# An NVFP4 MLP beside an ALiBi attention: weights turned by the crossbar instead of TensorE

## The chip, the cores and the metric

One core of one Trainium2 chip. The time is device microseconds of one execution. The profile is one more execution, and its trace names engines PE (TensorE), PEld (its weight loads), DVE (VectorE), ACT (ScalarE), POOL (GpSimd) and SP (SyncE, which here only issues transfers; SPq is its queue).

## The reference

x is 2048 x 512 in float32. It is normalised by layer norm to xn. The output is x + attention(xn) + mlp(xn). Attention has 16 query heads of 32 columns on 4 key and value heads, causal, with ALiBi slopes, softmax, and a projection Wo with a bias. The MLP has 4096 hidden columns; its three weight matrices come as 4-bit codes, two to an int32 word, with a float32 scale for each 32 columns:

```python
Wg = dequant_nvfp4(gate_W_packed, gate_scales)      # 4096 x 512
Wu = dequant_nvfp4(up_W_packed, up_scales)          # 4096 x 512
Wd = dequant_nvfp4(down_W_packed, down_scales)      # 512 x 4096
gate = jnp.einsum('th,nh->tn', xt, Wg)
up = jnp.einsum('th,nh->tn', xt, Wu)
gelu = jnp.tanh(0.7978845608028654 * (gate + 0.044715 * gate ** 3)) * gate * 0.5 + gate * 0.5
out = jnp.einsum('tn,hn->th', gelu * up, Wd)
```

## The kernel before, in words

**Numbers in two parts.** Matmuls of the MLP run in float16. A float32 value is held as a rounded part and the rest behind it (hi and lo, as in wh and wl, xh and xl, ih and il, phi and plo), and a product takes three matmuls: hi x hi, hi x lo, lo x hi. Attention scores run on float32 rows.

**Preamble** (function `preamble`). It normalises x, turns it, projects q, k and v in four chunks c of 512 tokens with five projections j each (j = 0 is k, 1 to 4 are q), stores them in DRAM, reads the scales, and decodes, turns and splits the first group of MLP weights. Its decode steps stand at (c, j) = (2, 4), (3, 0) and (3, 2). SP's program there is one sequence: the part stores of each projection (L538, L539), the v stores (L510), the loads for the first head (L499 to L503), and last the column scales (L554). The main loop begins when every engine has ended the preamble.

**Main loop** (function `main_loop`). 16 turns, called heads here: a turn i does attention head i and one group of 256 of the 4096 MLP columns. A head has 48 slots, and each engine walks through the slots by its own list, in order. The tables at the top say what stands in which slot. On TensorE a slot s holds: a score block (L1267, slots 6 to 44, `SCORE_AT`), up to two blocks of row maxima (L1245, up to slot 25), two halves of three MLP matmuls each (`PIECES`: gate, gate, down, up, up, down, L1213 and L1233), and in some slots a batch of probabilities times values (`VALUES_AT`, L1276: slots 12, 20, 28, 32, 40 and 47). The score blocks of slots 29 to 44 belong mostly to the last chunk of queries.

**The chain behind a score.** score_ps is one bank. TensorE writes it, DVE masks it where it lies on the diagonal, ACT takes the exponential into p (L1395, three buffers, `PR = 3`, so the exp of a block waits until POOL has read p of three blocks before), ACT rounds it to phi (L1402), and POOL subtracts to plo (L1668). The values batch of a slot waits for phi and plo of all its blocks; the batch of slot 47 for those of slot 44. POOL does, besides the plo splits: il (L1676, behind each up block, in slots 5, 11, ... 47), two adds of attention parts (L273, slots 19 and 23), their normalising (L279, slot 36) and onl (L291, slot 39).

**Weights of the next group.** In head i, group i + 1 is prepared. raw words are loaded by SP at the end of head i - 1 (L311). DVE decodes matrix m (0 gate, 1 up, 2 down) in five steps, one a slot, from slots 26, 31 and 36 (`DECODE_FROM`): two shifts (L319, L322), one mask over 1024 words (L326), and two multiplications by the scales (L334), which write wf, float32, 128 x 1024. There is one wf, so matrix m + 1 may write it only when m has been read. Then, in the slots of `TURN_W_AT` (31, 32, 36, 37, 41, 42), TensorE turns half of wf with four transposes of 128x128 (L347) into one of the two banks that the maxima used before, ACT copies it to wh (L354), and DVE subtracts to wl (L359). wh and wl have two buffers, one for each parity of i. The last head prepares nothing; DVE and ACT scale and split Wo there (ACT at slots 31 to 34).

```python
def turn_weights(pe, m, a, before, maxima):
    ...
    for k in range(KT):
        at = a * C + k * P if m < 2 else k * GROUP + a * P
        mm = nc.tensor.transpose(banks[a][:, k * P:(k + 1) * P], wf[:, at:at + P], ident[:])
    mm.then_inc(wturn_done, 1)
```

**SP in a head**: load_v and load_k for the next head; then for each chunk c, behind the last score block of the chunk: load_q of the next head (L1094, L1096) and gather_o of chunk c - 1 (L1151 to L1156), with the steps of the row sums at c = 0, 1 and 2 (spread_recips, L263, at c = 2); then load_raw for group i + 2, store_on and gather_o of the last chunk. The last block of chunk 2 is in slot 29, that of chunk 3 in slot 44. ACT copies o_ps and l_ps of a chunk (L1415, L1418), and lraw, of which there is one, waits for the store of the chunk before.

## Time and profile before

| what | value |
|---|---|
| median of 3 runs | 1736.85 us (1735.28 to 1737.32) |
| profiled execution | 1738.06 us |
| its span in the trace | 1736.2 us |
| busy: TensorE, VectorE, ScalarE, GpSimd | 1666.9, 1312.1, 1067.0, 935.9 us |
| preamble | up to about 123 us of the span |
| main loop, 16 heads | about 97 us each |
| middle head that is read closely | 707.2 to 804.5 us of the span |

The profile gives busy times by engine, groups of like instructions by line, who waited for whom, the chain that ended last, and a timeline. Matmuls overlap in it: a record of TensorE is longer than the time to the next one, so costs on TensorE are read from start to start.

### The profile page before, as it was taken

How to read it: one execution, taken by the hardware profiler on the slowest of the kernel's cores; microseconds unless marked ns; L12 is line 12 of the kernel's file. 1: busy time of each engine (PE TensorE's matmuls, PEld its weight loads, DVE VectorE, ACT ScalarE, POOL GpSimd, SP SyncE). 2: the span in 40 equal slices, each digit the busy share in tenths (PEclk: the TensorE clock that was granted, in tenths of full speed). 3: DMA queues.
4: the chain of work that ended last, by engine and by line, in shares of the span. 5: the costliest groups of instructions: out<-in, count | busy, mean ns of one | idle time of the engine just before them, and what ended most of it. 6: DMA issues, size and time to landing. Idle time of an engine off the chain costs nothing.

```text
span 1736.2 us, 30755 instructions
## 1 busy us (share of the span) xinstructions
PE 1666.9 (96%) x10337; PEld 830.9 (48%) x10337; DVE 1312.1 (76%) x2782; ACT 1067.0 (61%) x1788; POOL 935.9 (54%) x807
## 2 busy tenths in 40 slices
PE   4989999999999999999999999999999999999998
PEld 3764444444444444444444444444444444444443
DVE  6767778777777777777777778777777778777755
ACT  2336757575666757575766757575767657575650
POOL 3304637465665747465655747464656647464650
PEclk9999999999999999999999999999999999999999
DMA  6761020202021020202021020202020120202135
GB/s 195 197 188 44 15 74 18 76 26 71 18 62 38 23 79 17 75 27 75 17 72 26 26 76 17 75 27 76 18 76 19 28 74 17 76 27 82 32 102 181
DMA packets 95843, 106.86 MB, mean 62 GB/s; under 512 B 38288, under 2 KB 63768, under 8 KB 93992
## 3 DMA queue, kind: packets, MB, share of 16 engines
q1 hardware_dynamic: 91368, 99.27, 20.6%
q10 hardware_dynamic: 4320, 5.64, 1.0%
q8 instruction: 83, 1.36, 0.3%
q14 instruction: 72, 0.59, 0.1%
HBM read 69.60 MB, written 22.42 MB: 53 GB/s over the span
## 4 chain that ended last, share of the span: by engine, by line
PE 74%; DVE 8%; issue 6%; ACT 5%; DMA 0%; POOL 0%; SPq 0%; POOLq 0%; DVEq 0%; ACTq 0%
PE up_ps L1233 16%; PE down_ps L1213 16%; PE gate_ps L1233 15%; PE o_ps L1276 8%; PE score_ps L1267 8%; PE max_ps L1245 4%; PE turn_ps L1245 3%; ACT p L1395 2%; DVE mxp L1526 2%; PE l_ps L1276 2%; ACT wh L354 1%; PE max_ps L347 1%; DVE score_ps L1511 1%; DVE gl L1482 1%; DVE acc L1473 1%
## 5 line engine op out<-in xcount | busy, mean ns | idle before, releaser
L1668 POOL TENSOR_TENSOR plo<-p,phi 128x512 f16<-128x512 f32 (+1 forms) x576 | 661.0, 1158 | 317.6 <-ACT phi L1402 316.3
L1395 ACT ACTIVATE p<-score_ps,pshift 128x512 f32<-128x512 f32 (+1 forms) x576 | 381.5, 662 | 284.3 <-DVE score_ps L1511 154.7
L1676 POOL TENSOR_TENSOR il<-prod,ih 128x512 f16<-128x512 f32 x128 | 160.4, 1253 | 371.1 <-DVE ih L1505 371.1
L1402 ACT ACTIVATE phi<-p 128x512 f16<-128x512 f32 (+1 forms) x576 | 349.5, 607 | 15.2
L1267 PE MATMUL score_ps<-qst,kst 128*128 128x512 f32 (+3 forms) x640 | 308.0, 497 | 20.5 <-ACT p L1395 18.8
L1526 DVE TENSOR_REDUCE mxp<-max_ps 128x1 f32<-128x512 f32 x256 | 175.5, 686 | 52.2 <-PE max_ps L1245 52.2
L1473 DVE TENSOR_TENSOR acc<-down_ps,acc 128x512 f32<-128x512 f32 x237 | 161.8, 683 | 62.4 <-PE down_ps L1213 62.1
L1233 PE MATMUL gate_ps<-xh,wh 128*128 128x512 f16 x512 | 198.8, 388 | 0.0
L1233 PE MATMUL up_ps<-xh,wh 128*128 128x512 f16 x512 | 197.9, 387 | 0.0
L1213 PE MATMUL down_ps<-wh,ih 128*128 128x512 f16 x506 | 195.8, 387 | 0.0
L1233 PE MATMUL gate_ps<-xh,wl 128*128 128x512 f16 x512 | 194.8, 380 | 0.0
L1233 PE MATMUL gate_ps<-xl,wh 128*128 128x512 f16 x512 | 194.7, 380 | 0.0
L1233 PE MATMUL up_ps<-xh,wl 128*128 128x512 f16 x512 | 194.0, 379 | 0.0
L1233 PE MATMUL up_ps<-xl,wh 128*128 128x512 f16 x512 | 194.0, 379 | 0.0
L1213 PE MATMUL down_ps<-wl,ih 128*128 128x512 f16 x506 | 191.8, 379 | 0.0
L1213 PE MATMUL down_ps<-wh,il 128*128 128x512 f16 x506 | 191.8, 379 | 0.0
L1267 PEld LDWEIGHTS score_ps<-qst,kst 128*128 128x128 f32 x640 | 116.3, 189 | 117.1 <-ACT p L1395 51.8
L1276 PE MATMUL o_ps<-phi,vst 128*32 128x512 f16 (+3 forms) x1744 | 164.4, 348 | 0.0
L1245 PE MATMUL max_ps<-kst,qst 128*128 128x512 f32 (+2 forms) x320 | 151.7, 474 | 11.9 <-SPq L1099 5.5
L1245 PE MATMUL turn_ps<-kst,qst 128*128 128x512 f32 (+3 forms) x320 | 141.3, 441 | 0.4 <-DVE mxp L1522 0.3
L1276 PE MATMUL o_ps<-plo,vst 128*32 128x512 f16 (+3 forms) x1024 | 136.2, 342 | 0.0
L1379 ACT ACTIVATE gl<-gate_ps,cur 128x512 f32<-128x512 f32 x128 | 87.7, 685 | 69.4 <-issue 44.0
(301 smaller groups left out, 2836.0 us busy)
## 6 DMA issues: line engine op xcount, KB each, us to landing
qst<-q_parts SPq DMA_DIRECT2D x192, 64.0 KB
o<-oraw SPq DMA_DIRECT2D x192, 64.0 KB, 2.0
kst<-k_parts SPq DMA_DIRECT2D x45, 256.0 KB, 6.0
vst<-v_parts SPq DMA_DIRECT2D x16, 512.0 KB, 6.1
q_parts<-o SPq DMA_DIRECT2D x24, 256.0 KB, 3.4
acc<-in_L_attn_x_dram SPq DMA_DIRECT2D x4, 1024.0 KB, 7.5
raw<-L_ffn_gate_W_packed_dram SPq DMA_DIRECT2D x16, 256.0 KB, 3.0
raw<-n_L_ffn_up_W_packed_dram SPq DMA_DIRECT2D x16, 256.0 KB, 3.1
```

Source lines behind the costliest of these rows:

```text
L1213: mm = nc.tensor.matmul(dst[:], lhs, rhs, start=(q == 0), stop=(q == 5))
L1233: mm = nc.tensor.matmul(dst[:], lhs, rhs, start=(q == 0), stop=(q == 11))
L1245: mm = nc.tensor.matmul(dst[:, 0:cols], qst[:, c, t * P:(t + 1) * P], kst[par][:, m * CH:m * CH + cols], start=True, stop=True)
L1267: mm = nc.tensor.matmul(score_ps[:, col:col + width], kst[par][:, j * P:(j + 1) * P], qst[:, c, tok:CH], start=True, stop=True, skip_group ...
L1276: mm = nc.tensor.matmul(bank[g * HD:(g + 1) * HD, tok:CH], vst[:, j, of * HD:(of + 1) * HD], src[n % PP][:, col:col + CH - tok], start=sta ...
L1379: nc.scalar.activation(gl[a][:], gate_ps[:], ACT.Square, scale=cur[par][:, a:a + 1]).then_inc(square_done, 1)
L1395: nc.scalar.activation(p32[n % PR][:, 0:cols], score_ps[:, 0:cols], ACT.Exp, bias=pshift[:, 0:1]).then_inc(exp_done, 1)
L1402: nc.scalar.activation(phi[n % PP][:, 0:cols], p32[n % PR][:, 0:cols], ACT.Copy).then_inc(phi_done, 1)
L1473: nc.vector.tensor_tensor(acc[:, n % NT, :], bank[:], before, ALU.add).then_inc(acc_done, 1)
L1526: nc.vector.tensor_reduce(mxp[c % 2][:, t, m:m + 1], pair_ps[n % 2][:, 0:cols], AX.X, ALU.max).then_inc(red_done, 1)
L1668: nc.gpsimd.tensor_tensor(plo[n % PP][:, 0:cols], p32[n % PR][:, 0:cols], phi[n % PP][:, 0:cols], ALU.subtract).then_inc(plo_done, 1)
L1676: nc.gpsimd.tensor_tensor(il[w % 2][:, a, :], prod[a][:], ih[w % 2][:, a, :], ALU.subtract).then_inc(il_done, 1)
```

## The change

The float32 transposes of the MLP weights on TensorE go, with the copies out of PSUM behind them. Instead, for each matrix, ACT rounds the whole wf (128 x 1024) to float16 rows, which lie in the raw buffer just decoded (`rows_hi`); POOL subtracts them from wf to the rows behind them (`rows_lo`), which lie in the second part of o3; and SP issues two transposing DMAs (`turn_rows`), one for the hi rows into wh and one for the lo rows into wl, each 256 KB. In the main loop ACT does this in slots 31, 36 and 41, POOL in slots 32, 37 and 42, SP behind spread_recips of chunk 2. There is one buffer of lo rows, so POOL waits for the turn of matrix m - 1 before it writes those of m. The decode of m + 1 waits for POOL's read of wf. TensorE waits for the turned weights at its first use in a head. The scale that the copies of the down weights applied moves into the product on DVE (L1497). The packed down weights are loaded in two DMAs, in another order of columns. In the preamble, ACT has its copies at (2, 4), (3, 1) and (3, 4), POOL its three subtractions behind all its other work, and SP the turns at (3, 1), (3, 3) and before the last v store.

```diff
-TURN_W_AT = {31: (0, 0), 32: (0, 1), 36: (1, 0), 37: (1, 1), 41: (2, 0), 42: (2, 1)}
+ROWS_HI_AT = {31: 0, 36: 1, 41: 2}
+ROWS_LO_AT = {32: 0, 37: 1, 42: 2}
+W_DMAS = 2
...
-TURN_FIRST_AT = {(3, 0): 0, (3, 2): 1}
+ROWS_FIRST_AT = {(2, 4): 0, (3, 1): 1, (3, 4): 2}
+TURN_FIRST_AT = {(3, 1): 0, (3, 3): 1}
...
+    hi_rows = [t[:].bitcast(F16) for t in raw]
...
+        for a in range(2):
+            src = packed[2].rearrange("(k p) (g a w) -> g a p k w", p=P, a=2, w=GROUP // 4)[bass.ds(g, 1), a]
+            sp.dma_start(raw[m][:].rearrange("p (a k w) -> p a k w", a=2, k=KT)[:, a],
+                         src.rearrange("o p k w -> (o p) k w")).then_inc(raw_in[m], 16)
...
                 dve.wait_ge(dec_step, before * 9 + m * 3 + 3)
-                dve.wait_ge(wturn_done, before * 6 + 2 * m)
+                if m or before:
+                    dve.wait_ge(rowlo_done, before * 3 + m)
...
-    def turn_weights(pe, m, a, before, maxima):
...
-    def weights_hi(act, m, a, before, b):
...
-    def weights_lo(dve, m, a, before, b):
...
+    def rows_hi(act, m, before):
+        act.wait_ge(wf_done, before * 6 + 2 * m + 2)
+        nc.scalar.activation(hi_rows[m], wf[:], ACT.Copy).then_inc(rowhi_done, 1)
+
+    def rows_lo(pool, m, before, lo_row):
+        pool.wait_ge(rowhi_done, before * 3 + m + 1)
+        nc.gpsimd.tensor_tensor(lo_row, wf[:], hi_rows[m], ALU.subtract).then_inc(rowlo_done, 1)
+
+    def turn_rows(sp, m, before, b, lo_row):
+
+        for done, rows, dst in ((rowhi_done, hi_rows[m], wh[b]), (rowlo_done, lo_row, wl[b])):
+            sp.wait_ge(done, before * 3 + m + 1)
+            sp.dma_start_transpose(dst[:, m].rearrange("p a (k n) -> p (a k) n", n=P), rows).then_inc(w_in[m], 16)
...
+                        if (c, j) in TURN_FIRST_AT:
+                            turn_rows(sp, TURN_FIRST_AT[c, j], 0, 0, lo_rows[TURN_FIRST_AT[c, j]])
...
+                turn_rows(sp, 2, 0, 0, lo_rows[2])
                 store_v(NCH - 1)
...
                 nc.gpsimd.partition_all_reduce(rall, rmax, P, RMAX).then_inc(rall_done, 1)
+                for m in range(3):
+                    rows_lo(pool, m, 0, lo_rows[m])
...
+        lo_rows = [o[:, 1, :].bitcast(F16) for o in o3]
...
                         if i and c == 2:
                             spread_recips(sp, i - 1)
+                        if i < LAST and c == 2:
+                            for m, used in enumerate((gate_done, up_done, down_done)):
+                                sp.wait_ge(used, after(i * (GU if m < 2 else ND)))
+                                turn_rows(sp, m, i + 1, 1 - par, lo_rows[1 - par])
                     if i + 2 < HEADS:
                         for m in range(3):
-                            sp.wait_ge(wf_done, (i + 1) * 6 + 2 * m + 2)
+                            sp.wait_ge(w_in[m], 16 * W_DMAS * (i + 2))
                             load_raw(sp, m, i + 2)
...
+                            if n % ND == 0:
+                                pe.wait_ge(w_in[2], 16 * W_DMAS * (g + 1))
...
+                                if n == 0:
+                                    pe.wait_ge(w_in[m], 16 * W_DMAS * (i + 1))
...
-                        if s in TURN_W_AT and i < LAST:
-                            m, a = TURN_W_AT[s]
-                            turn_weights(pe, m, a, i + 1, (red_done, after((i + 1) * NMAX)))
...
+                        if s in ROWS_HI_AT and i < LAST:
+                            rows_hi(act, ROWS_HI_AT[s], i + 1)
...
-                        nc.vector.scalar_tensor_tensor(prod[a][:], gl[a][:], 0.5 * IS / (XS * WS) ** 2, up_ps[:],
+                        nc.vector.scalar_tensor_tensor(prod[a][:], gl[a][:], cur[par][:, 4 + a:5 + a], up_ps[:],
...
+                        if s in ROWS_LO_AT and i < LAST:
+                            m = ROWS_LO_AT[s]
+                            if i:
+                                pool.wait_ge(osum_done, 2 * i)
+                            else:
+                                pool.wait_ge(acc_done, after(1))
+                            if m:
+                                pool.wait_ge(w_in[m - 1], 16 * W_DMAS * (i + 2))
+                            rows_lo(pool, m, i + 1, lo_rows[1 - par])
```

## Rows read from the trace of the kernel before

**Rows 1.** The page: busy time of each engine, share of the span, instructions
```profile
PE 1666.9 (96%) x10337; PEld 830.9 (48%) x10337; DVE 1312.1 (76%) x2782; ACT 1067.0 (61%) x1788; POOL 935.9 (54%) x807
```

**Rows 2.** The chain that ended last: start us, length us, what (longest pieces)
```profile
215.26 2.59 PE up_ps L1233 x12
...
1578.31 2.59 PE up_ps L1233 x12
1675.17 2.59 PE up_ps L1233 x12
```

**Rows 3.** Timeline of TensorE in one head's last third: start us, length us
```profile
768.40 0.38 PE L1213 MATMUL down_ps<-wh,il 128*128 128x512 f16 x1
...
768.85 0.39 PE L1233 MATMUL gate_ps<-xh,wh 128*128 128x512 f16 x1
...
771.48 0.38 PE L1233 MATMUL gate_ps<-xl,wh 128*128 128x512 f16 x1
771.69 0.60 PE L347 MATMUL max_ps<-ident,wf 128*128 128x128 f32 x4
...
772.37 0.39 PE L1213 MATMUL down_ps<-wh,ih 128*128 128x512 f16 x1
...
787.75 0.50 PE L1267 MATMUL score_ps<-qst,kst 128*128 128x512 f32 x1 [0.82 <-ACT p L1395]
...
802.61 0.39 PE L1276 MATMUL o_ps<-phi,vst 128*32 128x512 f16 x2
```

**Rows 4.** Busy by stretch: length, PE, PEld, DVE, ACT, POOL, clock, DMA; middle, last head
```profile
774.34:800.97 26.63, 25.50 (x156) 12.53 (x154) 21.49 (x32) 21.23 (x37) 21.39 (x17) 1.00 0.06 16
1652.12:1676.22 24.10, 22.72 (x130) 9.62 (x129) 11.86 (x21) 19.99 (x34) 19.48 (x17) 1.00 0.14 45
```

**Rows 5.** Groups of the whole run, shapes apart: the splits on GpSimd and ScalarE
```profile
L1668 POOL TENSOR_TENSOR plo<-p,phi 128x512 f16<-128x512 f32 x512 | 612.6, 1206 | 285.9 <-ACT phi L1402 284.6
...
L1402 ACT ACTIVATE phi<-p 128x512 f16<-128x512 f32 x512 | 322.8, 630 | 13.2
...
L1668 POOL TENSOR_TENSOR plo<-p,phi 128x256 f16<-128x256 f32 x64 | 49.7, 777 | 31.7 <-ACT phi L1402 31.7
...
L1402 ACT ACTIVATE phi<-p 128x256 f16<-128x256 f32 x64 | 26.7, 416 | 2.0
```

**Rows 6.** Timeline of ScalarE in the same stretch
```profile
770.58 0.69 ACT L1395 ACTIVATE p<-score_ps,pshift 128x512 f32<-128x512 f32 x1 [0.19 <-PE score_ps L1267]
...
773.15 0.59 ACT L354 ACTIVATE wh<-max_ps 128x512 f16<-128x512 f32 x1
...
775.72 0.69 ACT L1395 ACTIVATE p<-score_ps,pshift 128x512 f32<-128x512 f32 x1
```

**Rows 7.** Groups of VectorE with GpSimd busy (774.3 to 801)
```profile
L334 DVE TENSOR_TENSOR wf<-dec,sc 128x512 f32<-128x512 f16 x4 | 4.7, 1204 | 0.0
...
L326 DVE TENSOR_SCALAR dec<-dec 128x1024 int32<-128x1024 int32 x2 | 2.2, 1082 | 0.0
```

**Rows 8.** Groups of VectorE with GpSimd idle (96 to 116)
```profile
L334 DVE TENSOR_TENSOR wf<-dec,sc 128x512 f32<-128x512 f16 x6 | 3.9, 689 | 0.1
...
L326 DVE TENSOR_SCALAR dec<-dec 128x1024 int32<-128x1024 int32 x3 | 2.1, 695 | 0.1
```

**Rows 9.** Timeline of the transfer queue at the preamble's end
```profile
107.46 1.75 SPq L539 DMA_DIRECT2D q_parts<-o  x1
109.25 2.25 SPq L510 DMA_DIRECT2D v_parts<-wh  x4
...
122.38 0.46 SPq L554 DMA_DIRECT2D column_scales<-acc  x1
```

**Rows 10.** Timeline of ScalarE at the preamble's end, in brackets its wait
```profile
116.31 0.60 ACT L717 ACTIVATE o<-proj 128x512 fp32r<-128x512 f32 x1 [3.85 <-DMA q_parts<-wl]
```

**Rows 11.** Transfers by line: size and median us to landing
```profile
o<-oraw SPq DMA_DIRECT2D x192, 64.0 KB, 2.0
...
acc<-in_L_ffn_up_scales_dram SPq DMA_DIRECT2D x1, 256.0 KB, 14.3
```

More of the change, by code:

```diff
@@ L215, in build @@
             wf_done = sem("wf_done")
[L216 to L218 removed]
+            rowhi_done = sem("rowhi_done")
+            rowlo_done = sem("rowlo_done")
+            w_in = [sem(f"w_turned{m}") for m in range(3)]
             preamble(nc, locals())
@@ L470, in preamble @@
         CLEARED = 3
-        load_raw, decode_step, turn_weights, weights_hi, weights_lo = weight_steps(nc, e, w_ps)
+        load_raw, decode_step, rows_hi, rows_lo, turn_rows = weight_steps(nc, e)
+        lo_rows = [t.bitcast(F16) for t in sraw]
         QSCALE = float(np.float32(1 / np.sqrt(np.float32(HD))))
@@ L724, in _ @@
                             root(c + 2)
-                        if (c, j) in TURN_FIRST_AT:
-                            for a in range(2):
-                                weights_hi(act, TURN_FIRST_AT[c, j], a, 0, 0)
+                        if (c, j) in ROWS_FIRST_AT:
+                            rows_hi(act, ROWS_FIRST_AT[c, j], 0)
                     act.wait_ge(v_sum, c + 1)
@@ L897, in _ @@
                                 decode_step(dve, DECODE_FIRST_AT[c, j], step, 0, 0)
-                for a in range(2):
-                    weights_lo(dve, 2, a, 0, 0)
                 values_lo(NCH - 1)
@@ L1023, in main_loop @@
         out_done = sem("out_done")
-        load_raw, decode_step, turn_weights, weights_hi, weights_lo = weight_steps(nc, e, pair_ps)
+        load_raw, decode_step, rows_hi, rows_lo, turn_rows = weight_steps(nc, e)
         (load_sums, row_sums, store_recips, spread_recips, add_parts, normalise, output_hi, output_lo
@@ L1102, in _ @@
                     sp.wait_ge(stored, 32 * NCH)
-                for m in range(3):
-                    load_raw(sp, m, 1)
                 def body(i, par, pair):
@@ L1114, in body @@
                     if i == 0:
+                        for m in range(3):
+                            sp.wait_ge(w_in[m], 16 * W_DMAS)
+                            load_raw(sp, m, 1)
                         sp.wait_ge(os_out, 16)
@@ L1167, in load_early @@
                     sp.wait_ge(wf_done, 6 * HEADS)
-                    sp.wait_ge(wturn_done, 6 * HEADS)
+                    sp.wait_ge(rowlo_done, 3 * HEADS)
+                    for turned in w_in:
+                        sp.wait_ge(turned, 16 * W_DMAS * HEADS)
                     for g in range(KVH):
```

78 lines of the change are left out of this document (19 added, 59 removed).

## The prediction

> **What bounds the kernel now.** I read the page first, then the chain, then one head's last third on each engine, then the preamble's end. On the page TensorE is busy 96% of the span [rows 1], so it looks like the bound everywhere, and the change takes work from it. The chain shows one mark per head, twelve up matmuls in a row: from 215.26 to 1578.31 there are 14 heads, 97.36 us each [rows 2]. The head behind them, the last, decodes and turns no weights, and still takes 96.86 us from mark to mark [rows 2]. So leaving the transposes out is not worth what they cost by themselves, unless the last head's own extras ate it. The reader should look for the engine that takes over. The timeline of TensorE shows it: at 787.75, between slots that hold the transposes, it sat idle 0.82 us for the exp on ScalarE [rows 3], and that exp may only run when GpSimd has read the p buffer of three blocks earlier (PR = 3). In the stretch from GpSimd's split of slot 32 to that of slot 44, 26.63 us, GpSimd is busy 21.39, TensorE 25.50 [rows 4]. This third of the head is where all added work goes; the other two thirds are untouched.
>
> **Removed from TensorE.** From the last matmul of slot 30 (768.40) to the first of slot 31 (768.85) pass 0.45 us, a score block between them. With four transposes as well, 771.48 to 772.37, it is 0.89 [rows 3]. A group of four costs 0.44 us (not the 0.60 of its record, which overlaps its neighbours). Six groups are 2.64 us a head, 15 heads 39.6 us. That is the ceiling of the gain. The six wl subtractions leave VectorE, which does not set this stretch's end; I count nothing for them. GpSimd is what may cover them.
>
> **Moved on ScalarE.** The two wh copies out of PSUM, 0.59 each [rows 6], become one copy of 128x1024 in SBUF. By the phi rows 256 more columns cost 630 - 416 = 214 ns [rows 5], so 1024 cost 630 + 428 = 1.06 us: the sum stays. But it all stands in slot 31, ahead of phi, where before half of it stood two slots later: phi and exp of slots 32 and 33 (exp at 775.72 [rows 6]) come 0.5 us later, and GpSimd's split of slot 32 starts at 774.84, not 774.34.
>
> **Added on GpSimd.** rows_lo has the form of the plo split at twice the width. 512 columns take 1206 ns, 256 take 777 [rows 5]: 1024 take 1206 + 2 x 429 = 2.06 us by slope, 2.41 by doubling; I take 2.2, so 6.6 us a head, all in slots 32, 37 and 42. Behind it queue the plo splits, and behind these the exps, the scores and, at slot 47, the last batch of values, which needs the plo of slot 44. TensorE began that batch at 802.61 [rows 3]. Today's GpSimd work of the stretch and the new: 21.39 + 6.6 = 28.0 us, from 774.84: plo 44 ends at 802.8. Without the transposes TensorE would be there at 802.61 - 2.64 = 799.97 and wait. So GpSimd becomes the bound, and the batch starts 0.2 us later than before.
> The lower bound takes GpSimd undisturbed, as in the last head, where the same 17 operations took 19.48 us [rows 4], and rows_lo at 2.06: 774.84 + 25.7 = 800.5, 2.1 us earlier. The upper bound comes from the decode. Beside GpSimd a wf multiply of VectorE takes 1204 ns and a mask 1082 [rows 7], alone 689 and 695 [rows 8]; GpSimd in turn pays 21.39 - 19.48 = 1.9 us. The decode steps of the stretch are 4 x 0.69, 2 x 0.70 and two shifts; with the shifts at no more than a mask each, 5.6 us. If GpSimd paid all of them: 19.48 + 5.6 + 3 x 2.41 = 32.3, end 807.1, 4.5 us later. Today GpSimd has 5.2 idle microseconds in the stretch for them to hide in; with no gaps left the 1.9 grows to some 1.9 / 0.8 = 2.4, which is +0.5 on the 0.2. The decode also waits for rowlo now, and rows_hi for the decode. I take +1.0 us a head, 15 us in all, nearest the sum of today's rows.
> The Trainium skill, "SBUF — State Buffer", section Who interferes with whom, has VectorE's two-port operations and GpSimd hold one port pair by turns for a whole instruction, the loser blocked. The trace agrees that both stretch, but shows GpSimd paying about a third of VectorE's length; by the rule in full the sum would be the upper bound above, 67 us instead of 15.
>
> **Added on the transfer queue.** Six transposing DMAs a head, issued by SP behind spread_recips. Issue: 0.46 to 1.75 us for one today [rows 9]; I take 0.6, and 0.46 to 1.75 for the range. Six are 3.6 us in a stretch in which SP only waits for scores. Behind the last of them stand load_q, gather_o and load_raw of the head's end; ScalarE's lraw copy waits for gather_o, and some microseconds at a head's start are free there. The down weights' load, now two DMAs, hides there too. TensorE's new waits for turned gate and up weights stand at a head's start, over 10 us behind slot 37's rows; the one for down weights stands eight slots into the head, so a turn issued at 803 has some 15 us. Landing: no row shows a transposing DMA. Between SBUF tiles 64 KB land in 2.0 us, and 256 KB in small pieces take 14.3 [rows 11]. GpSimd's rows_lo of m = 1 (slot 37, about 788) waits for the turn of m = 0, whose rows are ready at 778: up to some 9.5 us cost nothing, and I take that it is less, as a contiguous SBUF copy is the nearest.
> Two pages of the skill disagree here. "DMA: Bandwidth & Descriptors", section Latency and other measured facts, gives transposing DMAs 261 GB/s, an estimate of 1.0 us for 256 KB, which hides. "VectorE: DVE Perf Modes", section The three transpose paths, gives the crossbar 1309 ns for a 128x128 block against 390 on TensorE; eight blocks in a row would be an estimated 10.5 us for each DMA, which does not hide. No run here shows either.
>
> **The preamble.** Its end is set by SP, not TensorE: v stores, 4 in 2.25 us from 109.25, the last issue at 122.38 [rows 9], and ScalarE waited 3.85 us for a store before 116.31 [rows 10]. The 24 transposes there save nothing. Added: two turns at 0.6 us before the store that ScalarE waits for (+1.2, 117.5), its copy 0.5 behind that (1.06, to 119.1), rows_lo 2.2 (121.3), one turn (121.9), the v stores and the column store (2.7): 124.6 instead of 122.84, +1.8. At 1.75 us an issue, all six in SP's chain of 10.7 us of other work from 109.2: 130.4, +7.6. I take +4.
>
> **Sum.** 15 + 4 = +19 us. The profiled execution took 1738.06 (span 1736.2), 1.2 above the median of 1736.85; on the median's scale I forecast 1756.
>
> **Rivals.**
> Faster: GpSimd keeps up as in the last head. For it: 19.48 against 21.39 [rows 4], and fewer VectorE operations. Against: the last head has no decode, which now meets more GpSimd work. It gives 4 - 15 x 2.1 = -28, 1709; the ceiling is 4 - 39.6, 1701. It decides from where the added work costs GpSimd less than 802.61 - 774.84 - 21.39 = 6.4 us a head beyond today's, less 0.3 for the preamble's 4 us over 15 heads. Chance 0.23.
> Ports by turns: the upper bound, 4.5 a head, 67 + 4 to 8: about 1805; half of it 1775. For it: the record of wf grows by 0.5 us beside GpSimd. Chance 0.17 for +2.5 a head and more.
> Slow crossbar: a landing over 9.5 us. At 14.3, rows_lo of m = 1 starts at 792.4, ends at 794.6, lands at 808.9, rows_lo of m = 2 ends at 811.1, two plo 1.8: 812.9, +10.3 a head, near 1895. The 10.5 us of the skill's page, with hi and lo in a row, would give about 16 us a head, near 1980. Chance 0.10.
>
> **The numbers.** Forecast case (-0.5 to +2.5 us a head, 1733 to 1778) 0.50. A measurement of this kernel tells about 0.2%, 3.5 us. Faster takes the first rival and a sliver of the forecast case: 0.25. Same, 1733 to 1740, 0.08. Slower 0.67. The range leaves out the slow crossbar and the fastest tenth: 1715 to 1805.
>
> **What would show it.** Right: head marks 98 to 99 us apart; GpSimd without a gap in slots 32 to 44; a TensorE wait before the values of slot 47, named plo; rows_lo of 2.1 to 2.4 us. Wrong: marks at 95 us (GpSimd kept up), a GpSimd wait for a DMA on wh or wl at slots 37 and 42 (crossbar), SP issues of several microseconds, or TensorE waiting for gate weights at a head's start.

## The result, and the profile after

The changed kernel takes **1756.17 us** (median of 4 runs, 1754.83 to 1757.97) against 1736.76 for the kernel before on the same chip: ratio 1.0115, interval 1.0099 to 1.0131. It is 19 us slower. The profiled execution took 1755.9 us (span 1754.1); the trace of it splits the loss in two. One execution of the copy with the down rows at slot 45 took 2338.73 us at a mean granted clock of 0.656, and its median below leaves that one out.

The page after: busy time of each engine, the transfer queues, the chain that ended last by engine.

```profile
PE 1643.9 (94%) x9953; PEld 787.8 (45%) x9953; DVE 1274.1 (73%) x2686; ACT 1067.2 (61%) x1740; POOL 1043.9 (60%) x855
...
DMA packets 205666, 132.00 MB, mean 75 GB/s; under 512 B 156304, under 2 KB 173592, under 8 KB 203816
...
issue 42%; POOL 36%; PE 11%; DVE 2%; ACT 1%; POOLq 0%; DMA 0%; SPq 0%; DVEq 0%; ACTq 0%
```

TensorE has 384 instructions and 23 us of busy time less than in [rows 1], GpSimd 48 instructions and 108 us more. 36% of the chain that ended last is now GpSimd's. The number of DMA packets more than doubled (before 95,843).

The same marks of that chain as in [rows 2], and one more: the twelve up matmuls of the first head and of the last, and the up_ps of the final projection; in the second fence the last mark in the kernel before.

```profile
222.78 2.59 PE up_ps L1236 x12
...
1693.39 2.59 PE up_ps L1236 x12
...
1745.67 2.59 PE up_ps L1336 x12
```
```profile
1727.80 2.59 PE up_ps L1337 x12
```

In the kernel before, the first stands at 215.26 [rows 2]. So the first mark comes 7.5 us later, and the loop (first to last mark) takes 1522.89 us against 1512.54, **+10.35 us, 0.69 a head**. All the experiments below are read by this one difference; the times of whole kernels are compared with their own runs of the kernel before. The first mark stands near the end of the first head, so that head's own transposes and subtractions lie ahead of it.

The 7.5 us are there when the loop begins. The first matmul of the loop, in the kernel before and in the changed one:

```profile
123.62 0.45 PE L1245 MATMUL max_ps<-kst,qst 128*128 128x128 f32 x1 [5.51 <-SPq L1099]
```
```profile
131.19 0.45 PE L1248 MATMUL max_ps<-kst,qst 128*128 128x128 f32 x1 [8.37 <-SPq L1091]
```

Each stands 0.78 us behind the end of SyncE's last issue of the preamble, at 122.84 and 130.41. From there to the first mark pass 91.64 and 91.59 us.

One head, from one start of the last batch of values to the next, and in the second line the stretch from GpSimd's split of slot 32 to that of slot 44. First the kernel before, then the changed one; the columns are those of [rows 4].

```profile
705.29:802.61 97.32, 95.85 (x612) 46.43 (x611) 74.98 (x161) 64.12 (x107) 56.59 (x48) 1.00 0.17 46
```
```profile
716.75:814.83 98.08, 94.45 (x588) 43.74 (x588) 72.74 (x155) 64.14 (x104) 63.35 (x51) 1.00 0.27 62
786.17:814.68 28.51, 25.36 (x139) 10.52 (x137) 20.88 (x28) 20.84 (x34) 28.15 (x20) 1.00 0.31 55
```

TensorE is busy 1.40 us a head less and idle 2.16 more (3.63 against 1.47), which makes the 0.76 of this head. ScalarE's busy time is unchanged. GpSimd is busy 6.76 us more, and in the stretch it is busy 28.15 of 28.51 us, where it was 21.39 of 26.63 [rows 4]. The granted clock is at 1.00 in both, and plays no part in the loop.

The idle times of TensorE in this head, in brackets, with what ended them:

```profile
788.29 0.50 PE L1270 MATMUL score_ps<-qst,kst 128*128 128x512 f32 x1 [0.83 <-ACT p L1394]
795.68 0.49 PE L1270 MATMUL score_ps<-qst,kst 128*128 128x512 f32 x1 [0.95 <-ACT p L1394]
799.72 0.50 PE L1270 MATMUL score_ps<-qst,kst 128*128 128x512 f32 x1 [0.41 <-ACT p L1394]
807.46 0.51 PE L1270 MATMUL score_ps<-qst,kst 128*128 128x384 f32 x2 [0.47 <-ACT p L1394]
814.83 0.39 PE L1279 MATMUL o_ps<-phi,vst 128*32 128x512 f16 x2 [0.62 <-POOL plo L1662]
```

The kernel before had two such waits in this stretch, 0.82 [rows 3] and 0.31. The last line is the batch that [rows 3] shows without a wait at 802.61: now it waits for plo. Part of GpSimd's timeline leading up to it:

```profile
803.02 1.61 POOL L294 TENSOR_TENSOR onl<-o,onh 128x512 f16<-128x512 f32 x1
804.59 2.90 POOL L1662 TENSOR_TENSOR plo<-p,phi 128x512 f16<-128x512 f32 x2
807.46 1.16 POOL L1670 TENSOR_TENSOR il<-prod,ih 128x512 f16<-128x512 f32 x1
808.58 2.26 POOL L1662 TENSOR_TENSOR plo<-p,phi 128x512 f16<-128x512 f32 x2
810.82 2.12 POOL L353 TENSOR_TENSOR o<-wf,raw 128x1024 f16<-128x1024 f32 x1
812.91 1.77 POOL L1662 TENSOR_TENSOR plo<-p,phi 128x512 f16<-128x512 f32 x2
```

Not one line has a bracket: nothing is waited for. (In the whole stretch GpSimd has one gap, 0.36 us before an il at 792.92.) The subtraction of 810.82 stands right ahead of the plo that the batch needs.

The groups of the added work (busy, mean ns | idle before, releaser), and the transposing transfers with their median time to landing:

```profile
L342 DVE TENSOR_TENSOR wf<-dec,sc 128x512 f32<-128x512 f16 x96 | 110.2, 1162 | 29.8 <-POOL o L353 29.2
L353 POOL TENSOR_TENSOR o<-wf,raw 128x1024 f16<-128x1024 f32 x45 | 96.4, 2143 | 0.0
...
L349 ACT ACTIVATE raw<-wf 128x1024 f16<-128x1024 f32 x48 | 50.6, 1054 | 22.5 <-DVE wf L342 22.5
```
```profile
wh<-raw SPq DMA_TRANSPOSE x48, 3.1
...
wl<-o SPq DMA_TRANSPOSE x45, 2.8
```

The subtraction takes 2.14 us, ScalarE's copy 1.05. Two new waits have come with them: VectorE stands 29.2 us before wf until GpSimd has read the old one, ScalarE 22.5 us before its copy until VectorE has written wf (4.4 of them once, in the preamble).

### The profile page after: what moved, and what is told of

The parts are those of the page before. It is cut to its first block, busy times and chain, and to the rows that moved or that the text cites. A ratio compares the mean times of both kernels' runs of the same rounds, so it can differ in the third digit from the quotient of the medians.

```text
span 1754.1 us, 29968 instructions
## 1 busy us (share of the span) xinstructions
PE 1643.9 (94%) x9953; PEld 787.8 (45%) x9953; DVE 1274.1 (73%) x2686; ACT 1067.2 (61%) x1740; POOL 1043.9 (60%) x855
## 4 chain that ended last, share of the span: by engine, by line
issue 42%; POOL 36%; PE 11%; DVE 2%; ACT 1%; POOLq 0%; DMA 0%; SPq 0%; DVEq 0%; ACTq 0%
POOL plo L1662 28%; POOL o L353 2%; PE o_ps L1279 2%; PE down_ps L1214 2%; PE up_ps L1236 2%; PE gate_ps L1236 2%; POOL il L1670 2%; POOL o L276 1%; POOL onl L294 1%; PE score_ps L1270 1%; POOL o L282 1%; PE max_ps L1248 1%; DVE mxp L1522 0%; PE turn_ps L1248 0%; PE l_ps L1279 0%
## 5 line engine op out<-in xcount | busy, mean ns | idle before, releaser
L1662 POOL TENSOR_TENSOR plo<-p,phi 128x512 f16<-128x512 f32 (+1 forms) x576 | 671.1, 1178 | 250.3 <-ACT phi L1401 250.3
L1270 PE MATMUL score_ps<-qst,kst 128*128 128x512 f32 (+3 forms) x640 | 313.7, 506 | 43.4 <-ACT p L1394 41.7
L1507 DVE TENSOR_TENSOR score_ps<-score_ps,mask_st 128x128 f32<-128x128 f32 x256 | 69.2, 293 | 94.1 <-PE score_ps L1270 92.8
```

What stands on the lines that cost most here:

```text
L1270: mm = nc.tensor.matmul(score_ps[:, col:col + width], kst[par][:, j * P:(j + 1) * P], qst[:, c, tok:CH], start=True, stop=True, skip_group ...
L1507: last = nc.vector.tensor_tensor(score_ps[:, col:col + P], score_ps[:, col:col + P], mask_st[:], ALU.add)
L1662: nc.gpsimd.tensor_tensor(plo[n % PP][:, 0:cols], p32[n % PR][:, 0:cols], phi[n % PP][:, 0:cols], ALU.subtract).then_inc(plo_done, 1)
```

## The experiments

**Theory G**: GpSimd's nearly gapless train between slots 32 and 44 sets the loop. **Rivals**: H, the handing over of the one wf buffer between VectorE, ScalarE and GpSimd; S, the transfers and SyncE's queue. Ratios are to the kernel before on the same chip; "loop" is the difference of the marks to the kernel before's 1512.54 us.

| kernel | ratio | median us | loop |
|---|---|---|---|
| changed | 1.0115 [1.0099, 1.0131] | 1756.17 | +10.35 |
| subtraction on VectorE | 1.0045 [1.003, 1.006] | 1743.99 | +0.64 |
| subtraction of 16 columns | 0.9933 [0.9917, 0.9949] | 1724.49 | -19.98 |
| before, no transposes | 0.9942 [0.9927, 0.9957] | 1725.95 | -9.91 |
| before, subtraction added | 1.0033 [1.0022, 1.0043] | 1741.34 | +4.89 |
| down rows at slot 45 | 1.0071 [1.0054, 1.0088] | 1746.21 | +0.77 |
| preamble order | 1.0107 [1.0091, 1.0122] | 1752.69 | +10.54 |
| transposes twice | 1.0262 [1.0247, 1.0277] | 1779.81 | +15.40 |
| output split at 45, 46 | 1.0049 [1.0032, 1.0066] | 1741.65 | +0.29 |
| three edits together | 1.0046 [1.0034, 1.0059] | 1743.42 | +1.55 |
| the same, up rows on VectorE | 1.0046 [1.0032, 1.006] | 1743.23 | -0.21 |
| before, output split at 45, 46 | 0.9958 [0.9944, 0.9972] | 1729.20 | -7.28 |
| copies a slot later | 1.006 [1.0047, 1.0074] | 1749.89 | +9.13 |

What TensorE waits for over the whole run, in us, sorts these kernels:

| kernel | for exponentials | for plo | for wf |
|---|---|---|---|
| before | 18.8 | 0 | 0 |
| changed | 41.7 | 8.7 | 0 |
| subtraction on VectorE | 39.9 | 0 | 0 |
| subtraction of 16 columns | 20.9 | 0 | 0 |
| before, no transposes | 35.2 | 0 | 0 |
| before, subtraction added | 19.4 | 0 | 3.7 |
| down rows at slot 45 | 42.5 | 0 | 0 |
| output split at 45, 46 | 40.6 | 0 | 0 |
| before, output split at 45, 46 | 11.0 | 0 | 0 |

### The low rows on VectorE

```diff
                         if s in DECODE_AT:
                             decode_step(dve, *DECODE_AT[s], nxt, i + 1)
+                        if s in ROWS_LO_AT:
...
+                            rows_lo_dve(dve, m, i + 1, lo_rows[1 - par])
...
-                        if s in ROWS_LO_AT and i < LAST:
...
-                            rows_lo(pool, m, i + 1, lo_rows[1 - par])
```

> The changed kernel with rows_lo in the main loop on VectorE instead of GpSimd, in the same slots (32, 37, 42); the preamble's three stay on GpSimd. Theory G (GpSimd's three subtractions of 2.14 us make it the bound of a head's last third): GpSimd gets its gaps back, the wait of the values of slot 47 for plo goes, heads take 95 to 96.5 us instead of 98.0, and with the preamble's +7.5 us left in place the time is 1705 to 1730, likeliest 1717. Rival H (the hand-over of wf, one buffer between four engines, holds the decode and with it ScalarE, whoever subtracts): 1745 to 1756. Rival S (the transposing DMAs or the transfer queue): no change, 1753 to 1759.

The loop comes back to within 0.6 us of before, and the batch of values waits no more, so where the subtraction runs was the loss. Theory G had asked for 1705 to 1730 us, though, and got 1744: VectorE pays. The group, three of its instructions in one head, and what GpSimd did beside the first:

```profile
L357 DVE TENSOR_TENSOR o<-wf,raw 128x1024 f16<-128x1024 f32 x45 | 77.0, 1711 | 0.0
```
```profile
779.47 1.22 DVE L357 TENSOR_TENSOR o<-wf,raw 128x1024 f16<-128x1024 f32 x1
788.76 2.29 DVE L357 TENSOR_TENSOR o<-wf,raw 128x1024 f16<-128x1024 f32 x1
800.02 1.60 DVE L357 TENSOR_TENSOR o<-wf,raw 128x1024 f16<-128x1024 f32 x1
```
```profile
779.82 1.89 POOL L1675 TENSOR_TENSOR plo<-p,phi 128x512 f16<-128x512 f32 x1 [0.61 <-ACT phi L1405]
```

The first began with GpSimd idle and took 1.22 us; the plo that began beside it took 1.89, where most take 1.16. The second began with GpSimd at work, on an operation that ended 1.21 us later, and took 2.29. TensorE's waits for exponentials stay, 0.84, 0.93 and 0.71 us a head.

### The subtraction nearly taken away

The subtraction is cut to 16 columns, and the transpose for the low weights sends the hi rows, so that the transfers, the copy and the order stay. The high half of the MLP weights thus stands where the low half should.

```diff
-        nc.gpsimd.tensor_tensor(lo_row, wf[:], hi_rows[m], ALU.subtract).then_inc(rowlo_done, 1)
+        nc.gpsimd.tensor_tensor(lo_row[:, 0:16], wf[:, 0:16], hi_rows[m][:, 0:16], ALU.subtract).then_inc(rowlo_done, 1)
...
-        for done, rows, dst in ((rowhi_done, hi_rows[m], wh[b]), (rowlo_done, lo_row, wl[b])):
+        for done, rows, dst in ((rowhi_done, hi_rows[m], wh[b]), (rowlo_done, hi_rows[m], wl[b])):
```

> The changed kernel with rows_lo of 16 columns instead of 1024; the lo turn sends the hi rows again, so waits, hand-overs and transfers stay, and the MLP lacks its right lo weights. Theory G: the cost of GpSimd's work alone goes; 1705 to 1730, within 5 us of the run with rows_lo on VectorE. Rival H: most of the cost stays, over 1745. Rival S: no change.

This kernel keeps all six transposing transfers a head and all of ScalarE's copies, and its loop is 20.0 us under the kernel before. GpSimd's three subtractions alone therefore cost 10.35 + 19.98 = **30.3 us, 2.0 a head**, of the 6.4 us that they take. Everything else in the change, taken together, is a gain in the loop. The expected agreement with the run on VectorE, within 5 us, did not come: the two lie 19.5 us apart, so on VectorE the subtraction costs nearly as much as on GpSimd once the wait for plo is gone. The three subtractions of the preamble are cut to 16 columns here too, and the first mark stays at 221.92: they are not what the preamble lost.

### The kernel before without the transposes

Its transposes are left out in the loop, with wh and wl written as zeros there; the copies and subtractions behind them stay. The MLP of heads 1 to 15 is thus left out of the result.

```diff
+        if before == 0:
             for k in range(KT):
...
             mm.then_inc(wturn_done, 1)
+        else:
+            pe.sem_inc(wturn_done, 1)
```

> The kernel before with its transposes in the main loop left out (the semaphore is raised without them; wh and wl become zero there, so the MLP is wrong for all groups but the first). It measures what taking TensorE's work away is worth with nothing added. Ceiling 39.6 us (1697). Theory G, from the last head of the kernel before: ScalarE and GpSimd already limit the stretch, the gain is 1.0 to 1.8 us a head, 1710 to 1722. Rival T (TensorE is the bound throughout): 1697 to 1701.

Only 9.9 us come back, 0.66 a head, less than the 1.0 to 1.8 that was expected. TensorE's busy time in a head:

```profile
696.46:793.12 96.66, 94.00 (x588) 43.67 (x587) 74.84 (x161) 63.92 (x108) 56.56 (x49) 1.00 0.17 46
```

It falls by 1.85 us, to 94.00. That is less than what the transposes took from start to start, 0.44 us for each of the six groups or 2.64 in all, because every wait leaves the ends of records standing that otherwise lie under the next one. The 2.0 us that the head does not give back are waiting: TensorE now stands 0.44, 1.28 and 0.52 us before exponentials, where it had stood 0.82 and 0.31, and starts other scores a little later.

### The kernel before with the subtraction added

GpSimd gets three subtractions of 128x1024 in slots 32, 37 and 42, of data that nothing reads.

```diff
+                        if s in (32, 37, 42) and i < LAST:
...
+                            nc.gpsimd.tensor_tensor(o3[1 - par][:, 1, :].bitcast(F16), xl[:, 0, :].bitcast(F32),
+                                                    xh[:, 0, 0:2 * CH], ALU.subtract)
```

> The kernel before, transposes on TensorE and all, with one more subtraction of 128x1024 on GpSimd in slots 32, 37 and 42 of each head but the last; its result is not used and nobody waits for it. Theory G: GpSimd runs out of gaps, the batch of slot 47 waits for it, and a head takes 0.3 to 1.5 us longer: 1741 to 1760, likeliest 1747. Rivals H and S: GpSimd's gaps of 5.2 us hold it nearly all, at most 1739.

The loop is 4.9 us longer, with TensorE's transposes still in it. But the wait that theory G asked for, the batch of slot 47 for plo, is not there: the last plo ends at 803.52 and the batch starts at 803.69. What is new is a wait of the transposes for wf, once a head:

```profile
782.24 0.66 PE L347 MATMUL max_ps<-ident,wf 128*128 128x128 f32 x4 [0.24 <-DVE wf L334]
```

It starts 0.62 us behind the matmul before it, where the kernel before has 0.21: VectorE is late with wf, since its mask beside the subtraction takes 1.68 us in this head, where it took 0.69. The time fell in the expected range for another reason than the one given. The changed kernel has the same subtractions and no transposes, and is longer still. So once GpSimd has this work, taking the transposes from TensorE gives nothing. The 5.5 us between the two must lie in what else the change brings (one longer copy on ScalarE, the waits that tie the subtraction to wf, the transfers); they were not measured apart. In the table they stand as 22.3 us more of waiting for exponentials and 8.7 for plo.

### The down rows behind slot 45

```diff
-ROWS_LO_AT = {32: 0, 37: 1, 42: 2}
+ROWS_LO_AT = {32: 0, 37: 1, 45: 2}
```

> The changed kernel with GpSimd's subtraction of the down projection's rows moved from behind slot 42 to behind slot 45, past the last low probabilities that the values product waits for. Theory G (GpSimd's train of work between slots 32 and 44 is what sets the end of the stretch): the wait of 0.4 to 0.6 us of the product o_ps on plo goes in each of 15 heads, 0.3 to 0.7 us a head, so 1745 to 1752 us. Theory H (the vector engine's wait for wf, handed over by GpSimd, is what costs) and theory S (the transposing transfers and their queue cost): nothing moves, or the transposed rows land later and the next head's down projection waits, 1755 to 1760 us. The wait of o_ps on plo near 0 in all of them.

One number moves one of three subtractions behind the plo that TensorE waits for, and 9.6 us of the loop come back, 0.64 a head, which is the 0.62 us of the wait. This is the clearest evidence for G: the same work, in the same places but one. What remains are the waits for exponentials:

```profile
784.15 0.49 PE L1270 MATMUL score_ps<-qst,kst 128*128 128x512 f32 x1 [0.83 <-ACT p L1394]
...
803.33 0.50 PE L1270 MATMUL score_ps<-qst,kst 128*128 128x384 f32 x2 [0.48 <-ACT p L1394]
```

With the two between, 0.95 and 0.41, they are the four of the changed kernel, to 0.01 us. The line with o_ps is gone.

### The order in the preamble

```diff
-TURN_FIRST_AT = {(3, 1): 0, (3, 3): 1}
+TURN_FIRST_AT = {(3, 0): 0, (3, 2): 1}
...
-                turn_rows(sp, 2, 0, 0, lo_rows[2])
                 store_v(NCH - 1)
...
                 sp.dma_start(os_s.rearrange("r (k p) -> (r k) p", p=P), orows[0:2 * KT]).then_inc(os_out, 16)
+                turn_rows(sp, 2, 0, 0, lo_rows[2])
```

> The changed kernel with the crossbar transposes ahead of the loop placed otherwise on SyncE: those of the first two matrices one place earlier, those of the third behind the last stores of the preamble, so that no store of activations or column scales waits behind them. If the 7.5 us that the preamble lost are SyncE's queue (stores issued late behind the transposes), 4 to 6 us come back: 1750 to 1752 us, first up_ps near 217 to 219. If it is the work on GpSimd ahead of the loop (three subtractions of some 2.1 us) or the transposes' landing, at most 1 us comes back or some is lost: 1755 to 1759 us.

The first mark stands at 219.74, 3.0 us earlier, less than expected. And the mark has its own scatter: in the five kernels with the changed kernel's preamble it stood between 218.97 and 222.78 (mean 221.3), in the four with this order between 218.31 and 220.67 (mean 219.3), in the four with the preamble of before between 212.91 and 215.26 (mean 213.6). So the loss ahead of the first mark is 7.7 us and the order is worth about 2 of it. Where SyncE stands in the changed kernel, and in this one:

```profile
108.80 2.65 SPq L359 DMA_TRANSPOSE wh<-raw  x1
111.51 1.45 SPq L359 DMA_TRANSPOSE wl<-acc  x1
113.00 2.35 SPq L509 DMA_DIRECT2D v_parts<-wh  x4
...
129.97 0.44 SPq L556 DMA_DIRECT2D column_scales<-acc  x1
```
```profile
124.00 0.48 SPq L555 DMA_DIRECT2D column_scales<-acc  x1
124.53 1.28 SPq L359 DMA_TRANSPOSE wh<-raw  x1
125.85 1.34 SPq L359 DMA_TRANSPOSE wl<-acc  x1
```

The store of the column scales goes out 6.0 us earlier, the last transposes at the same time (124.53 against 124.74). The first mark follows the end of SyncE's sequence, whatever stands last in it: that end lies at 122.84 in the kernel before, 130.41 in the changed one and 127.19 in this one, and the first matmul of the loop at 123.62, 131.19 and 128.14; in each of the profiles it comes 0.8 to 1.0 us behind. From 107.95 on the changed kernel's SyncE issues without a pause, the six transposing DMAs for 9.9 us of it. So the preamble's loss is SyncE's queue, and the new order leaves the six issues (8.2 us) in it.

### Each transpose twice

Each transposing DMA is issued a second time to the same place, when the first has landed (n is 0 for the hi rows and 1 for the lo rows).

```diff
-W_DMAS = 2
+W_DMAS = 4
...
             sp.dma_start_transpose(dst[:, m].rearrange("p a (k n) -> p (a k) n", n=P), rows).then_inc(w_in[m], 16)
+            sp.wait_ge(w_in[m], before * 64 + 32 * n + 16)
+            sp.dma_start_transpose(dst[:, m].rearrange("p a (k n) -> p (a k) n", n=P), rows).then_inc(w_in[m], 16)
```

> The changed kernel with each crossbar transpose issued twice, the second when the first has landed, to the same place. It measures what the transfers themselves cost: twelve instead of six a head, some 15 us more of SyncE's time a head. Theory G: the loop does not feel them (they have nearly a slot more than they need), the preamble does, where each lies in a row of stores: loop +0 to +0.3 us a head, preamble +8 to +20 us, 1763 to 1780 us. Theory S (the transfers collide with the row-sum transfers and the shares of SBUF): the loop gives up another 0.7 us a head or more, 10 us and more in the loop, 1780 to 1810 us.

The preamble pays 19.7 us: each of six transposes there stands in SyncE's chain with its whole way to landing. The loop pays 5.05 us, 0.34 a head, for 15 us a head of SyncE's time and a share of the DMA engines that grows from 0.27 to 0.37. That is just over G's bound and half of what S asked for. TensorE's waits are those of the changed kernel (0.83, 0.94, 0.41, 0.49, 0.64). If a second set of six costs 0.34, the first should by estimate cost about as much, and the copy with the cut subtraction, which has the first set, is 20 us under before all the same. S falls as the main cause.

### The output's split moved, and its control

```diff
-OUTPUT_HI_AT, OUTPUT_LO_AT = 38, 39
+OUTPUT_HI_AT, OUTPUT_LO_AT = 45, 46
```

> The changed kernel with the split of the normalised output (output_hi, output_lo) moved from slots 38 and 39 to 45 and 46, which takes some 1.6 us of GpSimd's other work out of the stretch where it has no gap. Theory G: the lost 0.69 us a head comes back, up to 1.6 us where the train of work is what decides: -0.5 to -1.5 us a head, 1735 to 1749 us. Theories H and S: GpSimd's load is not it, and nothing moves, 1754 to 1758 us. Where the split is wanted sooner than slot 46 by its reader, a new wait shows there and eats the gain.

10.1 us of the loop come back, as G wants. But the line moves work on two engines: GpSimd's onl, and ScalarE's onh, which stood in slot 38 among its exponentials. The control is the same line in the kernel before:

> The kernel before with only the split of the normalised output moved to slots 45 and 46, the control for that edit. In the kernel before the chain went over TensorE's own queue with GpSimd waiting for it, so theory G expects little: -3 to +1 us (1734 to 1738 by the median of 1736.8). If the move helps by itself, whatever the weights do (the rival), it gives some 10 us here too: 1725 to 1730 us, and then the gain of that edit says nothing about the change.

It gives 7.3 us there too, ratio 0.9958: 0.4% of the time of before lay in this order and has nothing to do with the change. My expectation for it was wrong, and without it the move would have been booked as proof of G. With the move in both, the change costs 7.6 us in the loop, where it cost 10.35.

The two gains of the move are near in size, but by the traces they are not the same gain. In the changed kernel the wait for plo went (8.7 us) and those for exponentials stayed (41.7, then 40.6). In the kernel before no batch waited for plo, and the waits for exponentials fell from 18.8 to 11.0. The wait of 0.82 us [rows 3] became 0.29, and ScalarE, which works without a gap ahead of that exponential, no longer has this there:

```profile
784.88 0.63 ACT L285 ACTIVATE onh<-o 128x512 f16<-128x512 f32 x1
```
```profile
782.20 0.50 PE L1267 MATMUL score_ps<-qst,kst 128*128 128x512 f32 x1 [0.29 <-ACT p L1395]
```

From the exponential before it to this one pass 2.74 us with onh between them and 2.18 without. So the kernel before lost its 7.3 us to ScalarE's queue; that GpSimd was near its limit there is not shown.

### Three edits together, and the up rows on VectorE

The down rows at slot 45, the output's split at 45 and 46, and the preamble's order.

> The changed kernel with the three edits together: the down projection's low rows behind slot 45, the split of the normalised output in slots 45 and 46, and the other order of SyncE's transposes ahead of the loop. Alone in the loop the first gave back 9.6 us and the second 10.1 us. Theory G (GpSimd's train between slots 32 and 44 sets the stretch, 0.69 us a head over before): together they take 2.1 + 1.6 us out of it; where GpSimd is then no longer the last, ScalarE and the vector engine set the floor that the copy with the cut subtraction showed (20 us under before in the loop), so 12 to 20 us back in the loop, 2 to 3 us of the preamble: 1734 to 1741 us. A rival (both edits remove the same single wait, the one of 0.6 us in front of the value products, and what is left is another engine's): not additive, 10 us back in the loop: 1742 to 1745 us.

The rival was right: the edits do not add up, 8.8 us come back and not 12 to 20, with some microseconds of the preamble (first mark at 218.44). One head of it, and TensorE's waits there:

```profile
705.65:802.99 97.34, 94.32 (x589) 43.67 (x587) 73.26 (x155) 64.31 (x105) 63.29 (x52) 1.00 0.28 62
```
```profile
780.32 0.49 PE L1270 MATMUL score_ps<-qst,kst 128*128 128x512 f32 x1 [0.83 <-ACT p L1394]
787.70 0.49 PE L1270 MATMUL score_ps<-qst,kst 128*128 128x512 f32 x1 [0.95 <-ACT p L1394]
...
799.48 0.50 PE L1270 MATMUL score_ps<-qst,kst 128*128 128x384 f32 x2 [0.84 <-ACT p L1394]
```

The second copy of it, with one of the three subtractions on VectorE:

```diff
+POOL_LO = (0, 2)
...
+                        if s in ROWS_LO_AT and ROWS_LO_AT[s] not in POOL_LO:
...
+                            rows_lo_dve(dve, m, i + 1, lo_rows[1 - par])
```

> The same three edits, and the subtraction of the up matrix's low rows (slot 37) on the vector engine in place of GpSimd. On the vector engine it takes 1.22 us alone and 2.29 beside GpSimd's work. If GpSimd's train still sets the stretch, 0.3 to 1 us a head comes back over the three edits alone: 5 to 15 us less than they. If the train is no longer the last, the vector engine pays: 0 to 10 us more than they.

The same time, 1743.23 against 1743.42: what GpSimd gives back VectorE takes (2.28 us for each of the 15). Five kernels with quite different loads of GpSimd now lie between 1741 and 1747 us, each with 97.3 to 97.4 us a head and TensorE waiting for exponentials on ScalarE. Only the copy with the cut subtraction lies below, with 96.0 us a head and the same copy on ScalarE.

### The copies a slot later

In the kernel with the three edits ScalarE stood idle 0.88 and 0.72 us before its copy, waiting for wf, with phi and the next exponentials behind it:

```profile
785.50 1.06 ACT L349 ACTIVATE raw<-wf 128x1024 f16<-128x1024 f32 x1 [0.88 <-DVE wf L342]
...
797.23 1.06 ACT L349 ACTIVATE raw<-wf 128x1024 f16<-128x1024 f32 x1 [0.72 <-DVE wf L342]
```

```diff
-DECODE_FROM = {26: 0, 31: 1, 36: 2}
+DECODE_FROM = {26: 0, 31: 1, 37: 2}
...
-ROWS_HI_AT = {31: 0, 36: 1, 41: 2}
-ROWS_LO_AT = {32: 0, 37: 1, 45: 2}
+ROWS_HI_AT = {31: 0, 37: 1, 43: 2}
+ROWS_LO_AT = {32: 0, 38: 1, 45: 2}
```

> The kernel with the three edits together, and in it the up matrix's copy and subtraction and the down matrix's whole train a slot later: decoding of the down matrix from slot 37, ScalarE's copies at slots 31, 37 and 43, GpSimd's subtractions at 32, 38 and 45. With the three edits alone ScalarE stands 0.88 us and 0.72 us a head before the copy, waiting for the vector engine's wf, with exponentials behind it, and TensorE waits 0.95 us for such an exponential. Theory A (what is left of the loss in the loop, 97.35 us a head against 96.8 of the kernel before with the same move of the output, is this wait of ScalarE): the waits before the copies vanish, TensorE's 0.95 us falls to 0.5 or less, 0.4 to 0.9 us a head, 6 to 13 us: 1730 to 1737 us. Rival B (it is the copy's own 1.05 us in one piece, which stays): TensorE waits as long at another place, 1741 to 1746 us. Rival C (the vector engine now waits longer for GpSimd's subtraction, with products of the feed-forward behind it): 1745 us and more.

Rival C fits. The waits before the copies went, from 28.6 us with the three edits to 4.4 (one wait, in the preamble), and the 0.95 us of TensorE became 0.54; but VectorE's wait for the subtraction grew from 29.2 us to 47.1, and the loop by 7.6 over the three edits, with new waits of 0.48 and 1.22 us for exponentials in a head (the latter was 0.84). The five executions lie at 1745.3 us (two) and 1749.9 to 1750.2 (three), and the trace is of one of the latter, so the 7.6 is the upper end. Two groups of this kernel, and one wf of a head:

```profile
L342 DVE TENSOR_TENSOR wf<-dec,sc 128x512 f32<-128x512 f16 x96 | 96.7, 1010 | 47.7 <-POOL o L353 47.1
...
L349 ACT ACTIVATE raw<-wf 128x1024 f16<-128x1024 f32 x48 | 50.3, 1048 | 4.4 <-DVE wf L342 4.4
```
```profile
796.08 1.57 DVE L342 TENSOR_TENSOR wf<-dec,sc 128x512 f32<-128x512 f16 x1 [3.21 <-POOL o L353]
797.56 0.73 DVE L1493 SCALAR_TENSOR_TENSOR prod<-gl,cur,up_ps 128x512 f32<-128x512 f32 x1
```

The product of the feed-forward stands in program order behind this wf and starts 3.21 us late with it. So theory H was not empty: with one wf buffer, VectorE, ScalarE and GpSimd hand it round, and a slot given to one is taken from another. A second wf buffer would cut this; it was not tried.

No kernel with the change came below the kernel before. The fastest complete kernel of the study is the one before with the output's split moved, 1729.20 us.

## Why the prediction was right

The forecast was 1756 and the measurement 1756.17. Two of its terms were off in opposite directions, 4.7 us too much in the loop and 3.5 too little in the preamble, so the agreement of the sum to 0.2 us is luck.

- **TensorE, 2.64 us a head as ceiling.** The price is right: all six groups of this head add 0.44 us from start to start, not only the one of [rows 3]. What became of it is not. The forecast had TensorE ready for the last batch at 799.97 and waiting 2.8 us for plo; measured, it is ready 97.46 us after the batch before (97.32 in the kernel before) and waits 0.62. The 2.64 us had gone ahead of that, into waits for exponentials, as they did without any work added (0.66 us a head back, not 2.64).
- **The exponentials behind GpSimd.** The prediction put the 0.82 us at 787.75 down to ScalarE waiting until GpSimd had read p. ScalarE had no gap there, and its waits for plo were 11.2 us over the whole run before and 11.3 after. It was ScalarE's own queue, as the control with the output's split showed. This reading was wrong, and with it the belief that GpSimd alone stood behind TensorE.
- **ScalarE, the copy 1.06 us, slot 32's split 0.5 us later.** The copy took 1.05. The split of slot 32 started 69.42 us behind the last batch of values instead of 69.05: 0.37 later.
- **GpSimd, 2.2 a piece, train of 28.0 us, +0.5 for the neighbours.** The pieces took 2.14, between the slope's 2.06 and the doubled 2.41. The train of 20 operations is 28.15 busy in 28.51 us, and the batch waits for it 28.66 us after its start; forecast 802.8 + 0.5 - 774.84 = 28.46. The gap that was to close closed, and the wait came where it was named, on plo before slot 47, 0.62 us.
- **The allowance for decode and handing over.** From +0.7 to the +1.0 a head that I took; measured 0.76 in this head and 0.69 on average. The loop's term was 15 us and measured 10.35. The waits of the handing over were there (29.2 and 22.5 us), but mostly beside other waits.
- **Ports by turns.** By [rows 4, 7, 8] GpSimd paid about a third of VectorE's length. It paid little again: 2.14 us a piece in the loop, and 2.14 in the kernel before with the subtraction added. VectorE paid: the mask of the decode took 932 ns a piece in the kernel before, 1194 in the changed one and 1253 in the kernel before with the subtraction added. One of them, begun while GpSimd's subtraction of 787.28 had 1.12 us to go:

```profile
788.30 1.67 DVE L333 TENSOR_SCALAR dec<-dec 128x1024 int32<-128x1024 int32 x1
```

Its own 0.69 and the 1.12 make 1.81. The 2.29 us above stand against 1.22 + 1.21, the 1.60 against 1.22 + 0.52, and the 1.89 us of plo against 1.16 and the 0.87 that VectorE had to go. All four times the engine that came second took its own length and the rest of the other's, less 0.14. So the rule of the Trainium skill, "SBUF — State Buffer", section Who interferes with whom, holds in these rows; the +67 us came from letting GpSimd pay for every decode step, where mostly VectorE came second.
- **The transfer queue, 0.6 an issue.** Half of what it was: 1.23 us in the median in the loop and 2.06 at most, 1.30 to 2.65 in the preamble. In the loop SyncE had the time, as forecast. Landing took 3.1 and 2.8 us in the median and 7.0 at most, below the 9.5 that were free, so the Slow crossbar did not come. The 1309 ns a block of "VectorE: DVE Perf Modes" in the Trainium skill would be an estimated 10.5 us; eight blocks landed in 3.1 with the issue in it. No wait for turned weights shows on TensorE in the loop. (The 16 us a head that the prediction names beside that figure do not follow: its own steps with 21 us for hi and lo give over 20. Nothing rested on it.)
- **The preamble, +4.** 7.5 in the profiled pair, 7.7 over all kernels, at the upper end (7.6) that was worked out for issues of 1.75. That end was the right one: at 1.75 us an issue it put SyncE's last issue at 130.4, and it ended at 130.41, with 1.65 us an issue. Here the term was mis-sized by nearly half, and it made up what the loop's term had too much.

So the core was right, GpSimd's train ending last before slot 47 and SyncE's queue ending the preamble; the way there was in part not. The one kernel that tests the core of the loop moves a single subtraction from slot 42 to 45 and gets 9.6 of the 10.35 us back. What the prediction did not see is how near the floor below lies: in five kernels that relieve GpSimd the head still takes 97.3 to 97.4 us. ScalarE's copy is not that floor, since the head takes 96.0 with it where the subtraction is cut to 16 columns. What holds the 97.3 is the subtraction itself, wherever it runs: on GpSimd it keeps wf, and ScalarE stands before its copy; on VectorE it delays what ScalarE reads. The two were not measured apart.

## What to carry to other kernels

Before work goes from the busiest engine to one that looks 54% busy, count that engine's train in the stretch in question, operation by operation, and ask whose input stands last in it: 6.4 us of new work a head cost 2.0 us, and where a single piece of it stood was worth 0.6. Test a placement that seems to undo a loss in the kernel before as well, and compare the waits, not only the times: here the move gave 10.1 and 7.3 us, through two different engines. Of work taken from the busiest engine ask which wait will grow in its place: of 2.64 us a head 0.66 came back. Of a transposing transfer count the issue on its queue, more than twice that of a plain one, as well as its landing, above all where stores wait behind it.

## What the runs showed that I had not expected

- Issuing a transposing DMA of 256 KB kept SyncE 1.23 us in the median in the loop, where plain ones of 256 KB, the loads of raw, took 0.43 to 0.59. It landed in 3.1 us in the median. The changed kernel has 110,000 packets more than the one before; doubling the transposes raised the DMA share of a head from 0.27 to 0.37 and cost TensorE 0.34 us a head, with no wait longer than before by more than 0.02 us. Where the 0.34 lie is not shown.
- A subtraction of 128x1024 on VectorE took 1.22 us where GpSimd was idle at its start, and 2.29 and 1.60 where it was busy; on GpSimd the group's mean was 2.13 to 2.15 us in every kernel, and 0.23 at 16 columns.
- Four float32 transposes of 128x128 cost TensorE 0.44 us from start to start, six times alike, though their record shows 0.60 us [rows 3] and the busy time of a head fell by only 0.31 for each four left out.
- In every profile the main loop's first matmul started 0.8 to 1.0 us behind SyncE's last issue of the preamble.
